# Expert stage with tokens on partitions: one matmul that centres, turns and gives logits; the residual added in the last sweep

## The reference, cut to what matters

```python
x = x + conv_sweeps(ln_over_channels(x))      # rows down, rows up, columns forward, columns backward
t = tokens(x)                                 # 16 * 3600 tokens of 64 channels
n = (t - mean(t)) / sqrt(var(t) + 1e-5)       # over the 64 channels
probs = softmax(n @ router_w + router_b)      # 8 experts, the best 2, their weights made to sum to 1
t = t + sum_k top_p[k] * (n @ expert_w[top_i[k]] + expert_b[top_i[k]])

def sweep_step(carry, row):                   # 35 + 34 such steps over rows, 99 + 98 over columns
    return row + relu(conv1d(carry, w, taps=9, pad=4))
```

## Time and profile before

| | us |
|---|---|
| median of 3 runs | 1489.31 |
| lowest and highest | 1487.41, 1489.89 |
| the profiled execution's own time | 1490.23 |
| its span | 1488.4 |

### The profile page before, as it was taken

How to read it: one execution, slowest core, us unless ns; L and a number is a source line. 1 busy time by engine, 2 the same in 40 slices (tenths; PEclk the granted TensorE clock), 3 DMA queues, 4 the chain that set the end, 5 groups by cost and what they waited for, 6 DMA issues and landing times.

```text
span 1488.4 us, 30314 instructions
## 1 busy us (share of the span) xinstructions
PE 1417.2 (95%) x9398; PEld 1202.8 (81%) x9398; DVE 846.6 (57%) x1751; ACT 770.1 (52%) x2349; POOL 518.3 (35%) x444
## 2 busy tenths in 40 slices
PE   7899999999998999999999998989999999989997
PEld 5899999999998999999999997555565556555654
DVE  4787888655553222222222222677777777777776
ACT  5567677434343222222222223666777677776774
POOL 2466666000000000000000002366667666676666
PEclk9999999999999999999999999799999999999999
DMA  4111111000000000000000001011211121111101
GB/s 138 45 50 60 66 47 63 23 0 0 0 0 0 0 0 0 0 0 0 0 0 0 0 0 36 9 45 45 88 44 44 44 76 56 44 44 53 58 23 45
DMA packets 17659, 46.41 MB, mean 31 GB/s; under 512 B 3168, under 2 KB 3168, under 8 KB 17632
## 3 DMA queue, kind: packets, MB, share of 16 engines
q1 hardware_dynamic: 17488, 45.76, 8.9%
q10 hardware_dynamic: 144, 0.33, 0.1%
HBM read 31.33 MB, written 14.75 MB: 31 GB/s over the span
## 4 chain that ended last, share of the span: by engine, by line
PE 81%; ACT 7%; DVE 6%; issue 4%; DMA 0%; DVEq 0%; POOL 0%; POOLq 0%; ACTq 0%
PE twin L922 31%; PE twin L839 25%; PE twin L980 9%; PE twin L992 4%; PE twin L962 4%; PE twin L949 3%; ACT scratch L460 2%; PE twin L830 2%; PE twin L940 2%; PE twin L824 2%; DVE scratch L761 1%; DVE parts L701 1%; ACT late L460 1%; ACT lnv L436 1%; ACT rstd L438 1%
## 5 line engine op out<-in xcount | busy, mean ns | idle before, releaser
L922 PE MATMUL twin<-kbuf,late 128*128 128x136 f32 (+2 forms) x3940 | 457.2, 279 | 5.0 <-DVE kbuf L671 5.0
L922 PEld LDWEIGHTS twin<-kbuf,late 128*128 128x128 f32 x3940 | 457.0, 191 | 5.3 <-DVE kbuf L671 5.3
L839 PE MATMUL twin<-parts 128*128 128x384 f32 (+2 forms) x2070 | 394.8, 343 | 0.0
L839 PEld LDWEIGHTS twin<-parts 128*128 128x128 f32 x2070 | 373.1, 189 | 2.9 <-issue 2.5
L677 DVE SCALAR_TENSOR_TENSOR kbuf<-twin,act_buf 128x144 f32<-128x144 f32 x394 | 121.2, 308 | 336.4 <-PE twin L922 336.4
L282 POOL TENSOR_TENSOR act_buf<-act_buf,x_in 128x400 f32 (+1 forms) x72 | 74.4, 1038 | 660.4 <-ACT act_buf L418 660.4
L418 ACT ACTIVATE act_buf<-kbuf 128x144 f32 x394 | 127.1, 323 | 331.3 <-DVE kbuf L677 331.3
L980 PE MATMUL twin<-em,parts 64*128 64x512 f32 x1404 | 227.6, 429 | 4.4 <-ACT scratch L460 2.2
L289 POOL TENSOR_TENSOR scratch<-scratch 128x512 f32<-128x512 f32 x126 | 160.8, 1280 | 103.2 <-DVE scratch L761 53.2
L980 PEld LDWEIGHTS twin<-em,parts 64*128 64x128 f32 x1404 | 115.0, 186 | 57.3 <-issue 31.0
L761 DVE TENSOR_TENSOR scratch<-twin,scratch 128x512 f32<-128x512 f32 (+1 forms) x126 | 114.9, 912 | 29.5 <-PE twin L980 29.5
(11 more groups left out here) (100 smaller groups left out, 1520.3 us busy)
## 6 DMA issues: line engine op xcount, KB each, us to landing
x_in<-x SPq DMA_DIRECT2D x72, 400.0 KB, 3.7
result<-act_buf SPq DMA_DIRECT2D x36, 400.0 KB, 2.9
scratch<-L_conv_w_d ACTq DMA_DIRECT2D x1, 320.0 KB, 4.9
scratch<-L_conv_w_u SPq DMA_DIRECT2D x1, 320.0 KB, 6.5
late<-L_conv_w_r SPq DMA_DIRECT2D x1, 320.0 KB, 6.5
late<-L_conv_w_l SPq DMA_DIRECT2D x1, 320.0 KB, 7.1
ew<-L_ffn_expert_w SPq DMA_DIRECT2D x2, 128.0 KB, 6.2
eb<-L_ffn_expert_b SPq DMA_DIRECT2D x1, 256.0 KB, 4.6
```

The source lines that it names most:

```text
L839: last = mm(acc[:, lo:hi], vw[:, k, wpart, si], carry[:, cpart, g, lo + s * BG:hi + s * BG], start=first and si == 0, stop=final and si == ...
L922: last = mm(banks[CONV[g]][:, lo * BG:hi * BG], hw[:, k, si], kbuf[:, g, lo + s:hi + s].rearrange("p j b -> p (j b)"), start=si == 0, stop ...
```

## The change

Of a pair of rows, `tokens` on PE takes each tile of 128 tokens as the stationary operand and multiplies it by one constant matrix `cl_w` of 144 columns: 128 that subtract the mean and 16 that give the router's logits of both halves. The result has tokens on partitions, with 128 channels and 16 logits beside each other. Three tiles form a chunk (`TC` = 3; five chunks, `NCK`, the last with one tile). For each chunk, ACT squares the channels and copies all 144 columns of each tile to SBUF (`copy_tokens`), DVE sums the squares (`square_sums`), ACT takes Ln and Exp of at most 6 numbers per partition (`inv_std_tokens`), POOL multiplies logits and channels by the result (`scale_tokens`), PE turns the channels back (`channels`, one transposing matmul per tile), and ACT and DVE split that into two parts as before (`first_part`, `second_part`). `center_tokens`, `variance_tokens`, `logits` and `normalise` go. The first softmax step is now an addition of the bias, no longer a sum over the two parts.

Everything for pair now lies inside the region of pair j, at the tiles p = 0 to 8; there is no `ahead`. PE has one bank for `tokens` (`CT`) and one for `channels` (`TB`). The fill normalises pair 0 alone.

The residual is added in the backward column sweep: POOL, and no longer ACT, copies `kbuf` back in that sweep and adds x, which arrives as an extra input `x_col` laid out by columns, in 20 blocks of 5 columns into the same `x_in`. In the expert stage SP only stores. PE's regions are no longer a loop of the program but written out.

```diff
+    TC = 3
+    NCK = -(-TILES // TC)
+    TOKS = TILES * TN
+    CLW = P + 2 * E
...
+        COLS = 5
+        NBLK = W // COLS
+        x_blk = x_in[:, :, :, :].rearrange("p s c n -> p s (c n)")[:, :, 0:COLS * REG * HP // W].rearrange(
+            "p s (i g j b) -> p s i g j b", i=COLS, g=G, j=HP)
...
+        raw_logit = sm[:, 5]
+        xt = x_in[:, :, :, :].rearrange("p s c n -> p (s c n)")
+        tl = xt[:, 0:NCK * TC * CLW].rearrange("p (b t n) -> p b t n", b=NCK, t=TC)
+        sqt = xt[:, NCK * TC * CLW:TC * (NCK * CLW + 2 * P)].rearrange("p (b t n) -> p b t n", b=2, t=TC)
+        stat = sb("stat", [P, 3, 2, 2 * TC])
...
+        cl_w = sb("cl_w", [P, CLW])
+        center_w = cl_w[:, 0:P]
...
+        CT, TB = 4, 5
...
+        FILL_CT, FILL_TB = [4, 0, 1, 2, 3], [5, 7, 5, 7, 5]
...
+            def load_columns(k, slot):
+                sp.dma_start(x_in[:, slot].rearrange("p c n -> p (c n)")[:, 0:COLS * REG * HP // W], x_col[k]).then_inc(s_xc[slot], 16)
             for slot in range(2):
                 sp.wait_ge(s_d, CH * (HP - 1 + slot))
+                load_columns(slot, slot)
+            with sp.Fori(1, NBLK // 2) as i:
+                for slot in range(2):
+                    for g in range(G):
+                        sp.wait_ge(s_cb[g], W + 2 * COLS * (i - 1) + COLS * (slot + 1) - 1)
+                    load_columns(2 * i + slot, slot)
...
+            with sp.Fori(0, HP) as j:
                 store(j)
...
+            def copy_back(u, i, slot, w):
+                for g in range(G):
+                    pool.wait_ge(s_k[g], u + 1)
+                    nc.gpsimd.tensor_tensor(cols[:, :, g, w], kbuf[:, g], x_blk[:, slot, i, g], ALU.add).then_inc(s_cb[g], 1)
+            def columns(k, slot, visit, count=COLS):
+                pool.wait_ge(s_xc[slot], 16 * visit)
+                for i in range(count):
+                    copy_back(k * COLS + (W - 1 + i), i, slot, k * -COLS + (W - 1 - i))
+            for slot in range(2):
+                columns(slot, slot, 1)
+            with pool.Fori(1, NBLK // 2 - 1) as k:
+                for slot in range(2):
+                    columns(2 * k + slot, slot, k + 1)
+            columns(NBLK - 2, 0, NBLK // 2)
+            columns(NBLK - 1, 1, NBLK // 2, COLS - 1)
+            for g in range(G):
+                t = cols[:, :, g, 0]
+                nc.gpsimd.tensor_tensor(t, t, x_blk[:, 1, COLS - 1, g], ALU.add).then_inc(s_cb[g], 1)
...
+            def scale_tokens(j, slot, c):
+                n, b, k = NCK * j + c, (slot + c) % 2, len(tiles_of(c))
+                inv = stat[:, 2, b, 0:2 * k].rearrange("p (t q) -> p t q", q=2).unsqueeze(3)
+                lg = raw_logit[:, 2 * TC * c:2 * TC * c + 2 * k].rearrange("p (t q) e -> p t q e", q=2)
+                xl = tl[:, c, 0:k, P:].rearrange("p t (q e) -> p t q e", q=2)
+                xn = tl[:, c, 0:k, 0:P].rearrange("p t (q c) -> p t q c", q=2)
+                pool.wait_ge(s_cp, n + 1)
+                pool.wait_ge(s_r2, n + 1)
+                if c == 0 and later(j):
+                    pool.wait_ge(s_sm, SMN * (j - 1) + 1)
+                nc.gpsimd.tensor_tensor(lg, xl, inv.to_broadcast([P, k, 2, E]), ALU.mult)
+                nc.gpsimd.tensor_tensor(xn, xn, inv.to_broadcast([P, k, 2, C]), ALU.mult).then_inc(s_xn2, 1)
...
+            def region(j, slot, now):
                 for p in range(TILES):
...
-            with act.Fori(1, W) as u:
+            with act.Fori(1, W - 1) as u:
                 copy_back(u, u)
...
+            def copy_tokens(j, slot, c, bank=CT):
+                n, b, k = NCK * j + c, (slot + c) % 2, len(tiles_of(c))
+                src = banks[bank][:, 0:TC * CLW].rearrange("p (t n) -> p t n", t=TC)[:, 0:k]
+                act.wait_ge(s_ct, n + 1)
+                if later(n - 1):
+                    act.wait_ge(s_vr, n - 1)
+                if later(j):
+                    act.wait_ge(s_tb, n - NCK + 1)
+                act.activation(sqt[:, b, 0:k], src[:, :, 0:P], ACT.Square).then_inc(s_sq2, 1)
+                act.activation(tl[:, c, 0:k], src, ACT.Copy).then_inc(s_cp, 1)
+            def inv_std_tokens(j, slot, c):
+                n, b, k = NCK * j + c, (slot + c) % 2, len(tiles_of(c))
+                act.wait_ge(s_vr, n + 1)
+                if later(n - 1):
+                    act.wait_ge(s_xn2, n - 1)
+                act.activation(stat[:, 1, b, 0:2 * k], stat[:, 0, b, 0:2 * k], ACT.Ln, bias=eps_c[:, 1:2], scale=1.0 / C).then_inc(s_ln2, 1)
                 act.wait_ge(s_ln2, n + 1)
+                act.activation(stat[:, 2, b, 0:2 * k], stat[:, 1, b, 0:2 * k], ACT.Exp, scale=-0.5).then_inc(s_r2, 1)
+            def first_part(j, slot, c, bank=TB):
+                n, k = NCK * j + c, len(tiles_of(c))
+                act.wait_ge(s_tb, n + 1)
                 if c == 0 and later(j - 1):
                     act.wait_ge(s_p, TILES * (j - 1))
...
+            def region(j, slot, now):
                 for p in range(TILES):
...
+            for c in range(NCK + 2):
+                if c < NCK:
+                    copy_tokens(0, 0, c, FILL_CT[c])
+                if 1 <= c <= NCK:
+                    inv_std_tokens(0, 0, c - 1)
                 if c >= 2:
+                    first_part(0, 0, c - 2, FILL_TB[c - 2])
+            exponential(0)
...
+                nc.vector.tensor_copy(cl_w[half, P + q * E:P + (q + 1) * E], ew[half, E * C:]).then_inc(s_em, 1)
+            nc.vector.tensor_copy(bias_row, eb[:, E * C:]).then_inc(s_em, 1)
...
+            def square_sums(j, slot, c):
+                n, b, k = NCK * j + c, (slot + c) % 2, len(tiles_of(c))
+                dve.wait_ge(s_sq2, n + 1)
+                if later(n - 1):
+                    dve.wait_ge(s_ln2, n - 1)
+                nc.vector.tensor_reduce(stat[:, 0, b, 0:2 * k], sqt[:, b, 0:k].rearrange("p t (q c) -> p (t q) c", q=2),
+                                        AX.X, ALU.add).then_inc(s_vr, 1)
+            def second_part(j, slot, c, bank=TB):
+                n, k = NCK * j + c, len(tiles_of(c))
+                dve.wait_ge(s_th, n + 1)
+                span = slice(TC * TN * c, TC * TN * c + TN * k)
+                nc.vector.scalar_tensor_tensor(tok[:, slot, 1, span], banks[bank][:, 0:TN * k], 1.0, tok[:, slot, 0, span].bitcast(F32),
                                                ALU.add, ALU.subtract).then_inc(s_tl, 1)
...
-                    lambda: v.tensor_reduce(logit_row, banks[LOG][:, 0:2 * NSM].rearrange("p (t l n) -> p t n l", l=2, n=2 * E), AX.X, ALU.add),
+                    lambda: v.tensor_tensor(logit, raw_logit, bias_row.unsqueeze(1).to_broadcast([P, NG, E]), ALU.add),
...
-                            dve.wait_ge(s_lt, j + 1)
+                            dve.wait_ge(s_xn2, NCK * (j + 1))
...
+                            gate_tile(j, slot, p)
+                            if now is not None:
+                                if 1 <= p < NCK + 1:
+                                    square_sums(now, 1 - slot, p - 1)
+                                if 4 <= p < NCK + 4:
+                                    second_part(now, 1 - slot, p - 4)
+                        if part == 2:
+                            add_behind(j, p)
...
+            for c in range(NCK + 2):
+                if c < NCK:
+                    square_sums(0, 0, c)
+                if c >= 2:
+                    second_part(0, 0, c - 2, FILL_TB[c - 2])
+            for p in range(TILES):
+                for part in range(3):
+                    softmax(0, 0, (p, part))
...
+            def tokens(j, slot, c, bank=CT):
+                n = NCK * j + c
+                if later(n):
+                    if bank == CT:
+                        pe.wait_ge(s_cp, n)
+                flat = cols[:, j].rearrange("p g w b -> p (g w b)")
+                for i, p in enumerate(tiles_of(c)):
+                    last = mm(banks[bank][:, CLW * i:CLW * (i + 1)], flat[:, tile_lo(p):tile_lo(p) + TN], cl_w[:, :],
+                              start=True, stop=True)
+                last.then_inc(s_ct, 1)
+            def channels(j, slot, c, bank=TB):
+                n = NCK * j + c
+                pe.wait_ge(s_xn2, n + 1)
+                if bank == TB:
+                    if later(n):
+                        pe.wait_ge(s_tl, n)
+                elif c >= 2:
+                    pe.wait_ge(s_tl, n - 1)
+                for i, p in enumerate(tiles_of(c)):
+                    last = mm(banks[bank][:, TN * i:TN * (i + 1)], tl[:, c, i, 0:P], ident[:, :],
+                              start=True, stop=True, is_transpose=True)
+                last.then_inc(s_tb, 1)
...
+                n, span = TILES * j + p, slice(TN * p, TN * (p + 1))
+                if p % TC == 0:
+                    pe.wait_ge(s_tl, NCK * j + p // TC + 1)
...
+            def region(j, slot, now):
                 for p in range(TILES):
+                    experts(j, slot, p)
                     if now is not None:
...
```

(45 more changed lines are left out.)

246 lines of the change are left out of this document (56 added, 190 removed).

## The result

| | before | after |
|---|---|---|
| median of 4 runs, us | 1488.46 | 1520.38 |
| lowest and highest | 1487.41, 1489.89 | 1516.92, 1521.62 |
| the profiled execution's span | 1488.4 | 1519.7 |
| first gating of pair 0 | 945.70 | 938.92 |
| first gating of pair 17 | 1459.58 | 1492.11 |

After is 2.1% slower: the ratio is 1.0211, 95% interval 1.0198 to 1.0224. The forecast was 1520 us.

What follows compares the result with a forecast made beforehand. PE was taken to bound the region before, waits after the change. First gating 938.1, plus 17 x (32.0 + 0.4), plus 1, plus 28.8 gave a span of 1518.7 us; forecast 1520 us, range 1500 to 1540 (0.56).

Steps and rivals of the forecast that it cites:

- the walk: Expert stage: one region's waits followed from engine to engine in six steps, summing to 32.0 us against 30.3 before.
- step 1: DVE alone: gates tiles 11, 12, 0 and 1, softmax steps, an `add_out`, then `square_sums(0)` with its hand-over: 7.3 us.
- step 2: ACT's Ln and Exp 0.45, gating of tile 2 1.6, Square 0.41, copy 0.55: 3.0 us; `tokens(3)` waits for the copy.
- the ring: From tile 4: `channels` waits for DVE's previous second part, behind gating that waits for PE; 10.1 us to experts 7.
- The waits are hidden: Expert stage: DVE's second part is done when PE comes to `channels`; region 28.4 us, time 1452 us; chance 0.10.
- The clock swings in every region: The ring on PE: two half-clock tiles a region, not a quarter of one; 44 us more, 1564; chance 0.22.
- POOL bound nothing: POOL's scaling off the path at 1.15 us a chunk; rival, its last-sweep copy binds: 49 us more, 1569, chance 0.04.

Runs made afterwards that it cites:

- e4: The kernel before with only the residual moved to the last sweep, added by POOL; normalisation and expert stage as before: 1490.2 us, ratio 1.0005.
- e1: The changed kernel with DVE's `second_part(p - 4)` ahead of `gate_tile(p)` instead of behind it, no instruction added: 1460.22 us, 0.9805 of the kernel before.
- e8: The changed kernel with ACT helping to gate tiles 0, 1, 6 to 10 and 12 instead of 2, 4 to 10: 1583.7 us, 1.0625 of before.
- e3: The changed kernel with one more POOL multiplication of each chunk, its result used nowhere: 1522.11 us, 1.0228 of the kernel before.
- e10: e1 with `channels` of chunks 2 and 4 put into the bank of `tokens` as well: 1463.79 us, 0.983 of the kernel before.

## Why the prediction was right

From step to step, in the region around 1133 us (start to start; what was predicted stands first):

| step | predicted | measured |
|---|---|---|
| 1: DVE gates 11 to ACT's Ln of chunk 0 | 7.3 | 7.58 |
| 2: to `tokens(3)` | 3.0 | 3.17 |
| 3: to experts 4 | 1.75 | 1.70 |
| 4: experts 4 to 7 | 3.61 + 3.34 + 3.14 | 3.65 + 3.38 + 3.20 |
| 5: experts 7 to gate 7 | 1.0 | 1.01 |
| 6: gate 7 to gate 8, to gate 11 | 2.87 + 5.97 | 2.98 + 5.77 |
| sum | 32.0 | 32.44 |

The rows of steps 1 and 2 are in ACT's timeline:

```profile
1138.43 0.30 ACT L481 ACTIVATE stat<-stat,eps_c 128x6 f32<-128x6 f32 x1 [0.61 <-DVE stat L725]
1138.76 0.21 ACT L483 ACTIVATE stat<-stat 128x6 f32<-128x6 f32 x1
1139.00 1.75 ACT L506 ACTIVATE late<-twin,scratch 128x64 f32<-128x64 f32 x8
1140.59 0.54 ACT L473 ACTIVATE x_in<-twin 128x384 f32<-128x384 f32 x1
1140.96 0.59 ACT L474 ACTIVATE x_in<-twin 128x432 f32<-128x432 f32 x1
```

- **The waits** are those foreseen: `channels` behind DVE's second part four times a region, 1.34 to 1.54 us (predicted 1.3 to 1.5). `tokens(3)` waits 0.85 us as a matmul, 1.29 as a weight load; I had said about 1.5. One wait of PE the prediction hadn't named, the 1.08 us for `add_out`; its 8 us of idle time (7.7 measured) came out without it.
- **The clock allowance was wrong, and that the sum hit so closely is in part luck.** I had added 0.4 us a region for half clock in one region of four, on the strength of the earlier trace rows. Behind the first region there is none (965.84 to 1485.71 us, granted clock 1.00). Its place in the sum was taken by 0.4 us that the walk had too little. In step 1, 0.23 us are a wait that it had at nothing: DVE's gating of tile 0 stands idle once a region until PE's `sum_experts` is done. In step 2, ACT's Ln to its gating takes 0.57 us and not 0.45, and in the ring the three rounds take 0.14 us more. So 32.4 predicted, 32.54 measured over 17 regions, by two errors of opposite sign; with the clock at full speed in the forecast as well it would have been 7 us lower, some 1513 us.
- **The first region** takes 33.5 us (first gatings at 938.92 and 972.43), 1.0 more than the mean of those behind it, since PE comes out of the fill at half clock (experts take 1.65 us at 944.37 and 0.95 at 947.97). The prediction had 1 us for this.
- **PE's work** is 24.76 us a region, predicted 23.9; three tiles of `tokens` take 0.84 us and not 0.75 (and 13 transposes at 0.53 / 4 are 1.7, not the 1.8 written). It is not a term of the sum, since PE is not what the path waits for at most tiles.
- **The fill:** first gating at 938.92, predicted 938.1. PE ran at 0.73 of full speed in it, for which I had left up to 4 us in the bounds.
- **The last sweep:** POOL's copy takes 0.49 us, predicted 0.45, and costs nothing. e4 shows it by itself.
- **The last part** took 27.6 us from the last pair's first gating to the end, predicted 28.8, what it was before. PE's first wait in it, in the kernel before and in the changed one:

```profile
1461.54 1.09 PE L992 MATMUL twin<-ident,scratch 128*128 128x128 f32 x4 [1.69 <-DVE act_buf L769]
```
```profile
1494.08 0.63 PE L1022 MATMUL twin<-ident,scratch 128*128 128x128 f32 x4 [1.68 <-DVE act_buf L801]
```

  Before, half clock followed this wait (the sum takes 1.09 us); after, it did not, and DVE gates tile 2 only 3.61 us behind the first gating where it had been 4.74. That is 1.1 of the 1.2 us: the clock again, and not the change.
- **The sum:** 938.9 + 17 x 32.54 + 27.6 = 1519.7 us of span; predicted 1518.7.
- **The rivals.** "The waits are hidden" would have come near with two DVE instructions in the other order: it gave a region of 28.4 us, and e1 measured 28.9. "The clock swings in every region" didn't come to pass in the change; in e8, where the first two idle pieces of a region are half a microsecond longer, it came in nine regions of 16. POOL bound nothing (e3). By the rule that I cited from the Trainium skill, "TensorE: Matmul & The Clock Gate", section "A second HAM failure mode: psum-queue depth-cycling", it should have swung here too. The change's trace, with idle pieces of 1.34 to 1.68 us, doesn't agree; e8's, with 1.9 to 2.1 us, does in the regions that fell and not in the others.

## What to carry to other kernels

Before work is taken off the busiest engine, walk the new waits as a cycle: a buffer with one slot, whose reader stands in its engine's list behind something that waits for the writer's engine, makes the two engines take turns, and then the sum of their steps counts and not the larger load. Such a ring is opened by the order (the release ahead of what waits) or by a second slot, and having both brought nothing more here. Once it is open, what is left is found by asking of each tile which engine's list binds: moving the help to tiles at which the helper had nothing urgent was worth another 32 us.

## What the runs showed of the hardware

- The length of one idle piece of PE didn't tell whether half clock follows. In the expert stage of the changed kernel there are 69 of 1.34 to 1.68 us, four within 10 us in every region, all entered at full clock, and the clock fell behind none. In the kernel before it fell behind one of 1.35 us and one of 1.69 (1461.54), and not behind 15 others of 1.29 to 1.35. Pieces of 1.89 and 2.07 us in the places of the change's first two were followed by 1.2 GHz in some regions and not in others (e8), and of two of 1.6 us at the same tile one was and one wasn't (e10, 1221.35 against 1252.35). What decides it stays open. So the same wait can cost nothing or 4 us (37.97 against 33.64), from one region to the next, and a kernel with such waits shows it in its scatter: e8's four runs spread over 24 us, the change's over 5.
- Two dependent instructions of ACT on six numbers a partition take 0.30 and 0.21 us and start 0.33 us apart, nearly as much as passing 384 columns (0.37 us from Square to copy, 1140.59 to 1140.96).
